# A new order for the first batch's opening in an eight-batch attention and feed-forward kernel

## The reference

```python
def attn(query, ...):                       # 16 heads of 16, LEVELS = 4
    outs = [mha(query[:, ::2 ** lvl, :], in_proj_w[lvl], in_proj_b[lvl], out_w[lvl], out_b[lvl]) for lvl in range(4)]
    current = outs[-1]
    for lvl in (2, 1, 0):                   # linear upsampling, one linear layer, plus the finer level
        current = upsample_linear(current, outs[lvl].shape[1]) @ up_w[lvl].T + up_b[lvl] + outs[lvl]
    return current

x = layernorm(x + attn(x))
h = silu(x @ w1.T * s1) * (x @ w2.T * s2)
h = gelu(gelu(h @ h1.T * t1) @ h2.T * t2)
x = layernorm(x + h @ w3.T * s3)
```

## Time and profile before

| | |
|---|---|
| median of 3 runs | 3591.69 us (3589.08 to 3593.05) |
| the profiled execution | 3593.05 us, its span 3591.2 us |
| between span and time, in that execution | 1.85 us |
| mean granted TensorE clock | 0.979 of full speed |
| PE, DVE, ACT, POOL busy | 94%, 70%, 71%, 29% of the span |

### The profile page before, as it was taken

The page is one execution under the profiler, slowest core; times in us unless marked ns, Lnnn a source line. Parts: engine busy times, 40 slices in busy tenths (PEclk is TensorE's granted clock), DMA queues, the critical chain, the costliest instruction groups (busy, mean ns, idle before and its releaser), DMA issues. The chain is left out here.

```text
span 3591.2 us, 58399 instructions
## 1 busy us (share of the span) xinstructions
PE 3376.2 (94%) x20635; PEld 1395.0 (39%) x20635; DVE 2529.6 (70%) x4805; ACT 2532.6 (71%) x3266; POOL 1043.0 (29%) x1060
## 2 busy tenths in 40 slices
PE   6999899999999999999999989599999999999998
PEld 3333333333333333333333322244444454444444
DVE  5988989988998998998998989323333333333333
ACT  3899899889899889889889878444444444444443
POOL 3343643543553454454454442200000000000000
PEclk7999999999999999999999999799999999999999
DMA  5343333433433333333333332200000000000000
GB/s 182 109 143 117 121 89 102 125 95 101 122 100 99 113 114 96 115 104 103 106 113 99 112 95 64 76 1 13 23 14 13 13 13 13 13 24 13 13 13 13
DMA packets 237693, 269.85 MB, mean 75 GB/s; under 512 B 55876, under 2 KB 203460, under 8 KB 236768
## 3 DMA queue, kind: packets, MB, share of 16 engines
q1 hardware_dynamic: 228144, 257.10, 24.2%
q10 hardware_dynamic: 9216, 8.39, 0.7%
HBM read 159.75 MB, written 101.45 MB: 73 GB/s over the span
## 5 line engine op out<-in xcount | busy, mean ns | idle before, releaser
L960 ACT ACTIVATE a_probs<-a_p_s,a_unit_now 128x1024 f32<-128x1024 f32 x1360 | 1441.1, 1113 | 171.4 <-PE a_p_s L1285 167.2
L1066 DVE TENSOR_REDUCE a_part_max<-a_p_r 128x1 f32<-128x512 f32 x2048 | 1290.0, 679 | 112.3 <-PE a_p_r L1298 106.8
L1298 PE MATMUL a_p_r<-a_k_st,a_q_st 48*128 48x512 f16 (+2 forms) x2944 | 861.3, 374 | 96.7 <-DVE a_part_max L1066 47.0
L1657 PE MATMUL p_h<-f_h_hi,f_w_hi 128*128 128x512 f16 x2048 | 777.4, 380 | 4.5 <-issue 4.5
L1657 PE MATMUL p_h<-f_h_lo,f_w_hi 128*128 128x512 f16 x2048 | 777.2, 379 | 0.0
L1315 PE MATMUL a_p_o<-a_probs,a_v_aug 128*17 128x512 f32 (+2 forms) x5888 | 726.3, 573 | 1.0 <-ACT a_raw L970 0.2
L1285 PE MATMUL a_p_s<-a_q_st,a_k_st 50*128 50x512 f16 (+2 forms) x2944 | 644.8, 368 | 18.4 <-ACT a_probs L960 15.7
L1298 PEld LDWEIGHTS a_p_r<-a_k_st,a_q_st 48*128 48x128 f16 x2944 | 217.2, 94 | 979.6 <-DVE a_part_max L1066 657.2
L1519 ACT ACTIVATE f_h_f<-p_h,f_sc_now 128x512 f32<-128x512 f32 x256 | 176.0, 688 | 519.3 <-PE p_h L1657 519.3
L1066 DVE TENSOR_REDUCE a_row_max<-a_p_r 128x1 f32<-128x512 f32 (+2 forms) x672 | 417.9, 679 | 34.0 <-PE a_p_r L1298 32.9
L1466 POOL TENSOR_TENSOR f_rstd<-f_var_eps,f_minus_half 128x1 f32<-128x1 f32 x64 | 35.0, 548 | 1242.6 <-DVE f_var_eps L1612 1242.6
(11 more groups left out here) (157 smaller groups left out, 4418.9 us busy)
## 6 DMA issues: line engine op xcount, KB each, us to landing
qk_scratch<-a_qk_room SPq DMA_DIRECT2D x288, 128.0 KB
a_q_st<-qk_scratch SPq DMA_DIRECT2D x240, 96.0 KB, 2.5
a_w_lo<-wqkv_inner SPq DMA_DIRECT2D x30, 768.0 KB, 5.8
a_a_lo<-a_attn SPq DMA_DIRECT2D x448, 32.0 KB, 2.0
a_k_st<-qk_scratch SPq DMA_DIRECT2D x64, 192.0 KB, 3.8
a_o_lo<-wo_inner SPq DMA_DIRECT2D x24, 512.0 KB, 3.5
a_qk_room<-wf SPq DMA_DIRECT2D x23, 512.0 KB, 3.8
a_k_st<-qk_scratch SPq DMA_DIRECT2D x112, 96.0 KB, 2.4
```

The costliest lines, as they stand in the source:

```text
L960: act.activation(probs[:, s % 2, 2 * p:2 * p + 2, :], p_s[:, 2 * p:2 * p + 2, :], ACT.Exp, scale=unit_now[:, lvl:lvl + 1]).then_inc(exp_do ...
L1066: dve.reduce_max(out, src, AX.X).then_inc(max_read.sem, 1)
L1298: ins = pe.matmul(p_a[:, r * size:(r + 1) * size], q_st[rows_of(j, ROWS), query_at:query_at + 128], k_st[rows_of(j, ROWS), key_at:key_at + ...
L1657: ins = pe.matmul(out, a, c, start=first and n == 0, stop=last and n == len(terms) - 1)
```

## The change

Only numbers in `OPEN` change. No instruction is added or removed. The diff in full:

```diff
@@ -301,24 +301,24 @@
 OPEN = {
-    "acut": (21.39, 24.62,),
-    "attn": (7.47, 12.05, 16.4, 19.22, 19.71,),
-    "invert": (5.56, 6.51, 10.56, 17.83, 20.05,),
-    "neg": (-9.75, -6.34, -3.72, 4.12, 8.26, 12.16, 17.11, 18.15,),
-    "proj": (-60.79, -35.49, -33.31, -31.03, -24.96, -18.84, -7.77, -2.91, -1.79, -0.49, 0.56, 6.78, 9.61, 10.58, 20.59,),
-    "raw": (3.12, 5.06, 9.54, 13.4, 16.72,),
-    "span": (-61.97, -33.89, -8.81, -2.79,),
-    "spanned": (-47.49, -23.23, -9.47, -2.85,),
-    "spread": (5.84, 8.73, 9.47, 9.9, 14.97, 15.44, 19.41, 19.54, 20.41, 20.7,),
-    "stack": (-31.18, -23.14, -14.98, -14.33, -8.92, -3.27, 7.16, 8.19, 16.08,),
-    "turn": (4.8, 5.01, 5.01, 6.73, 10.34, 10.55, 15.2, 15.81, 19.31, 19.85,),
-    "unit": (1.34,),
-    "v": (-34.29, -30.1, -29.69, -8.94, 5.57, 9.56, 15.85, 20.36,),
-    "wcut": (-65.25, -39.53, -10.43, -4.45,),
-    "wload": (-109.08, -93.47, -28.52, -7.23,),
-    "x": (-165.67, -151.2,),
-    "xcopy": (-5.93, 5.34, 32.88, 37.15, 38.05, 42.72, 68.92, 23.4,),
-    "xcut": (-75.1, -40.39,),
+    "acut": (10.4, 18.4,),
+    "attn": (4.75, 6.75, 10.75, 14.75, 18.75,),
+    "invert": (4.05, 6.05, 10.05, 14.05, 18.05,),
+    "neg": (-9.15, -7.15, -3.15, 0.85, 4.85, 8.85, 9.85, 17.85,),
+    "proj": (-28, -27, -16, -15, -14, -13, -5.7, -1.35, -0.15, 1.05, 2.25, 3.45, 4.65, 5.85, 7.05,),
+    "raw": (3.3, 5.3, 9.3, 13.3, 17.3,),
+    "span": (-30.7, -19.65, -7, -1.98,),
+    "spanned": (-30.65, -19.6, -6.95, -1.93,),
+    "spread": (4.35, 4.65, 6.35, 6.65, 10.35, 10.65, 14.35, 14.65, 18.35, 18.65,),
+    "stack": (-25.6, -24.6, -12.6, -12.5, -10.6, -10.5, -3.3, 4.5, 14,),
+    "turn": (3.55, 3.85, 5.55, 5.85, 9.55, 9.85, 13.55, 13.85, 17.55, 17.85,),
+    "unit": (0.1,),
+    "v": (-27.5, -15.5, -14.5, -5.45, 10.6, 11.6, 12.6, 13.6,),
+    "wcut": (-31, -19.95, -7.3, -2.28,),
+    "wload": (-36, -25.9, -10.9, -5.2,),
+    "x": (-36.01, -35.98,),
+    "xcopy": (1, 4.2, 7.4, 10.6, 13.8, 17, 20.2, 23.4,),
+    "xcut": (-33, -27,),
 }
```

## The result

| | before | changed |
|---|---|---|
| median, 4 runs each, timed together | 3592.37 us (3589.08 to 3596.02) | 3617.15 us (3616.00 to 3620.61) |
| ratio | | 1.0068, 95% interval 1.0052 to 1.0085 |
| profiled execution, its span | 3593.05, 3591.2 us | 3614.32, 3612.5 us |
| ACT's copy of the first transpose of the feed-forward part (L1481) | 2315.8 us | 2336.7 us |

The change costs 24.8 us, in a range of 19 to 31. Between the two profiled executions it is 21.3 us, and 20.9 of them are there when the attention part ends; the feed-forward part takes 1275.8 us after and 1275.4 before, from that copy to the end. The forecast was 3601.2 us with a range up to 3614: the direction was right, the size too small.

What follows compares the result with a forecast made beforehand. Attention bound by waits until 93 us, by DVE, then PE, from 100 us. 2.3 + 1.2 + 3.0 + 3 = 9.5 us on the profiled 3593.05 gives 3602.6, less 1.4: 3601.2 us; likeliest case 3594 to 3609, whole range 3588 to 3614.

Steps and rivals of the forecast that it cites:

- A: Opening up to projection 2: `w_lo` behind the scale product delays level 1, x1's load hidden; +2.3 us (1.6 to 3.2).
- B: Projections 2 to 5 up to the first maximum: stacks between projections wait for stores to land; +1.2 us (0 to 2).
- C: First maximum to `value0`: the new order walked task by task, `value0` 2.2 us later, plus projection 10; +3.0 us (1 to 5).
- M: Start of the first maximum, forecast at 46.7 us; times behind it are counted from there.
- The late load: Level 3's weights, loaded 11 us later, land near 56 us, ahead of their use at 58.7: just hidden.
- D: Steps behind `value0`: earlier projections and value tiles, ACT waiting for store landings; +3 us (0 to 6.6).
- The fast clock: Rival: unbroken maxima 0 to 19 let PE hold 2.4 GHz from 46 to 95 us; 3588.4 us, chance 0.18.
- The jam: Rival: SP's queues jam, stores land in 5.2 us among the eight copies, `wload2` no longer hidden; 3607 to 3614 us, chance 0.16.

Runs made afterwards that it cites:

- e8_x1_behind: Kernel before with only the load of x's second half moved behind `wload0` and the big weight copies; 3594.21 us, ratio 1.0004.
- e9_cut_first: Changed kernel with the four scale products (`span`) behind their cuts again, as before the change; 3608.46 us, ratio 1.0047 to the kernel before.
- e15_middle_cut_first: Kernel before with only the middle (first maximum to `value0`) in the new order, but cuts of levels 3 and 0 ahead of scale products; 3598.60 us, ratio 1.0018.
- e10_load_early: Changed kernel with level 3's weight load right behind projection 3's stores again; 3616.85 us, ratio 1.0065 to the kernel before.
- e7_proj_early: Kernel before with only projections 11 to 14 early, and the `neg` and `stack` tasks they need; 3600.24 us, ratio 1.0021.
- e4_copies: Changed kernel with the eight copies within DRAM back at their old times; 3616.20 us, ratio 1.0063 to the kernel before.
- e2_late_proj: Changed kernel with projections 11 to 14 back at their old times; 3611.61 us, ratio 1.0050 to the kernel before.
- e17_banks_worse: Kernel before, no task moved, with longer planned bank holding times so that 22 near reuses arise; 3599.80 us, ratio 1.0021.
- e16_banks_in_turn: Kernel before with projections 11 to 14 early, projection 11's copy moved ahead, and shorter planned holding times leaving no near bank reuse; 3604.02 us, ratio 1.0030.
- e18_all_repairs: Changed kernel with cuts ahead of scale products, copies of projections 10 and 11 moved ahead, and banks in turn; 3608.42 us, ratio 1.0045 to the kernel before.
- e5_late_steps_back: Changed kernel with everything due behind `value0` back at its old times; 3604.76 us, ratio 1.0033 to the kernel before.
- e13_copies_ahead: Kernel before with projections 11 to 14 early and an ACT sort edit that moved only projection 11's copy ahead; 3602.51 us, ratio 1.0029.
- e11_half_old_place: Kernel before with half the matmuls of batch 0's projections 11 to 14 left out, in their old places; 3587.07 us, ratio 0.9982.
- e12_half_early: Kernel before with batch 0's projections 11 to 14 early and half of their matmuls left out; 3595.63 us, ratio 1.0012.

## Why the prediction came out too low

**A, up to projection 2: +2.3 predicted, +3.15 measured.** 32.41 against 29.26 us. The mechanism was right (the port, the addition at 0.42 us, `w_lo` behind the scale product). The 0.9 us more is x1's load: I had it hidden, and ACT waited 0.89 us for it at 22.24, the upper bound I gave. By itself x1's place costs nothing (e8_x1_behind).

**B, to the first maximum: +1.2 predicted, +1.2 measured.** 47.58 - 32.41 = 15.17 us against 43.22 - 29.26 = 13.96.

**C, to `value0`: 54 us predicted, 57.4 measured (51.8 before).** This term was mis-sized: 2.2 against 5.6 us at `value0`, beyond its upper bound of 5. Up to `w_lo` of level 3 my walk holds: it ends at 66.27, M + 18.7, against M + 18.4. What failed stands in "projection 6 to M + 23.6, `max26`, `max27`, `v3` to M + 25.7". The load behind `v3` went at 75.88, M + 28.3. Projection 6 had to wait for six maxima until 67.37, then PE waited 0.78 us for the bank before `v3`. All later landmarks keep this lag: projection 7 at 89.50 (I had 86), `value0` at 105.00 (101). I let maxima, once queued, run at DVE's 0.61 us; the rows show two in banks, and a stop on both sides of a projection. The kernel before has that stop too, but its `v3` stands ahead of projection 6, so that the load of level 0 waits for no maximum behind projection 6. I also took POOL's new order as a cost at level 1 alone. With `span` behind the cuts again e9_cut_first gets 3.5 (profile) to 7.5 us (ratios) back, and e15_middle_cut_first 4 to 5 of the middle's 11 us. In C I had walked through that order and so had its cost in the sum, without seeing that it was a large part of it.

**The late load: hidden, as predicted.** e10_load_early changes nothing.

**D, the steps behind: +3 predicted (3.8 with the rest of projection 10, which C had), +11 measured** (from the 3rd to the 141st exponential 231 us against 220). This is the step that failed. I wrote that "DVE, the bound of this stretch, can only lose by gaps" and then priced only stores that ACT waits for. Such waits exist, at projections 13 and 14 as I wrote (0.58 and 3.14 us), and behind the longer one PE idles 1.92 us up to 134.45 and is at 1.2 GHz till 140. But e7_proj_early has none and still loses 7, and e4_copies shows that the copies within DRAM aren't what makes the stores late. What the runs showed in place of the gaps that I left at nothing is PE: in these steps it stands 7.5 us for DVE and 3.3 for ACT, against 4.0 and 0.7 before, and is busy 217.6 us against 212.1, of which projection 10 is 1.4 and part of the rest the low clock. The low clock isn't the main part: e2_late_proj and e17_banks_worse have a mean granted clock of 1.00 from the 3rd to the 141st exponential and take 227 and 228 us. What I didn't price is that the table's times also give out the banks. e17_banks_worse shows that a bank plan alone, with as many near reuses as the changed table makes, costs 7.5 us in this place. It isn't the whole account of the early projections: e7_proj_early has 9 near reuses and loses as much as e17_banks_worse with 22, and with the reuses gone (e16_banks_in_turn, e18_all_repairs) the time stays. What the runs exclude are the copies within DRAM, the value tiles and PE's matmul time as the whole cause. What fits them all is the lack of a free bank: in nearly every step a projection or a `neg` keeps one of three, and PE waits either for DVE (banks by the old holding times) or for ACT (banks in turn). Its rival is the place of ACT's copies of projections 12 to 14, which no run moved: copied sooner, they might let banks in turn work. That rival and a fourth bank weren't tried, and so this is argued and not shown. Nor is it settled how the last 3 to 5 us of D divide among `neg`, `stack`, the value tiles and the finishing tasks; in e2_late_proj, with them in the new places, 17 near reuses are left, and 11 in e5_late_steps_back.

**The sum.** In the profiled execution the terms missed by 0.9 (A), 0 (B), 3.4 (C) and 7.5 us (D), together 11.8; it took 3614.32 us where my sum said 3602.6, 11.7 more. The medians lie 24.8 us apart and not 21.3, because single executions of one kernel differ by some us. The upper bound of my sum was added wrongly: 3.2 + 2 + 5 + 6.6 is 16.8, not 17.2.

The Trainium skill (Perfetto Trace Analysis, section "Identifying Performance Opportunities") takes a gap that repeats on the engine which should be full as a sign that PSUM may have no room for the next tile. The trace agrees: 0.78 or 0.79 us stand in four of the changed kernel's PE rows above, though also in three of the kernel before.

**The rivals.** The fast clock didn't come: the middle has 0.55, as before, although 20 maxima ran unbroken. The jam came nearest in size, with an upper bound of 3614, and hardly by its cause: e4_copies and e10_load_early gain nothing. No repair that was tried makes the new order good: e18_all_repairs, with cuts, the copies of projections 10 and 11 and the banks changed, is still 16 us (0.0045) slower than the kernel before.

**The shares, by the 141st exponential:** front 5, middle 11 (`span` ahead of the cuts 5 of them), late steps 8 (projections 11 to 14: 5), less 2 that overlap: 22 us.

## What to carry to other kernels

When a table of times feeds more than one thing (here the order and the choice of banks), ask for each moved task what else its time decides. Count the near reuses of each bank by hand, before and after: a reuse at a distance of one or two could cost up to 0.8 us of PE here. Where two engines at 95% share three buffers, as in the steps here, price a task put between them by the stop on both sides, not by its own duration alone. And before a small product is moved ahead of a long one on the same engine, look at which of the two the next engine is waiting for. And when an edit is made to a sort key, print the order that comes of it: one offset less moved one copy here, where four were meant.

## What the runs showed of the hardware

The longest of PE's waits behind a projection for a bank that DVE still reads are 0.78 to 0.79 us (four rows of the changed kernel above), at 1.2 GHz and at 2.4 GHz alike, with 0.70 us of idle DVE on the other side at 65.23.

In nearly every case an idle time of PE of around 2 us that began at 2.4 GHz was followed by the low clock: 1.92 us up to 134.45 in the changed kernel, 2.04 us up to 91.42 in e7_proj_early, 94.47 in e13_copies_ahead, and twice in e16_banks_in_turn. The low stretch behind these lasts some 7 us though PE is busy for most of it. But 1.84 us in e9_cut_first left the clock at 1.00 from 127 to 134 us, and the clock also fell where no idle time was longer than 0.79 us: at 85.2 us in the kernel before and at 99.5 in the changed one. So the length of one idle time doesn't decide it. The three rows, of e9_cut_first, the kernel before and the changed one:

```profile
129.12 0.39 PE L1285 MATMUL a_p_s<-a_q_st,a_k_st 50*128 50x512 f16 x2 [1.84 <-ACT a_probs L960]
...
85.20:92.10 6.90, 6.12 (x23) 3.23 (x21) 3.46 (x6) 3.52 (x4) 1.15 (x1) 0.51 0.29 88
...
99.50:106.30 6.80, 6.01 (x35) 2.66 (x33) 3.48 (x6) 4.61 (x6) 1.57 (x2) 0.50 0.59 194
```

The Trainium skill (TensorE: Matmul & The Clock Gate, section "What's actually happening") describes the low clock as the default state from which activity releases the engine; the trace agrees in direction.

Behind the first maxima the clock first rises between 78 and 84 us in kernels whose tasks up to there are almost the same: at 78.3 in e8_x1_behind, 81.8 in the kernel before, 82.3 in e11_half_old_place, 83.2 in e17_banks_worse. In the kernel before it falls again from 85.2 to 92.1 us; in the other three it stays up beyond 160 us. Part of the 2 to 3 us by which single profiles differ at the 3rd exponential may come from there (93 in e7_proj_early, 96 in e12_half_early, which have the same tasks up to it); the last column of the table leaves it out.
